# A graph network kernel: the second edge sort is cut into counts, blocks beside the attention pass, and blocks behind it

## What is computed

```python
xn = layernorm(x)
# layer 0: sum over the edges at their source
agg0 = segment_sum(xn[dst] * edge_weight[:, None], src, num_segments=6250)
x = x + relu((xn + agg0) @ W1 + b1) @ W2 + b2 + linear_attention(xn)
x = x + expert_ffn(layernorm(x))
# layer 1: sum over the edges at their target
xn = layernorm(x)
agg1 = zeros.at[dst].add(xn[src])
x = x + (deg_isqrt * agg1) @ W + attention_layers(xn)
x = x + mixture_of_experts(x)
```

## Time and profile before

| what | us |
|---|---|
| median of the three runs | 6170.95 |
| the profiled execution: its own time | 6176.16 |
| its span in the trace | 6174.4 |
| the first sort's scatters on POOL, first and last start | 53.3, 1201.1 |
| DVE free of all earlier work | 1187.1 |
| the records landed, DVE goes on | 1207.82 |
| first gather of the first message stage | 1211.72 |

### The profile page before, as it was taken

One profiled execution on the slowest core, in us unless ns is written; L12 is line 12 of the kernel. 1 busy time (PEld: TensorE's weight loads), 2 busy tenths in 40 slices (PEclk: granted clock), 3 DMA queues, 4 the chain that ended last, 5 costly groups with the idle time before them and its releaser, 6 DMA issues.

```text
span 6174.4 us, 88136 instructions
## 1 busy us (share of the span) xinstructions
PE 5219.2 (85%) x24825; PEld 4400.5 (71%) x24825; DVE 3351.4 (54%) x9920; ACT 1347.2 (22%) x3057; POOL 3934.7 (64%) x4345
## 2 busy tenths in 40 slices
PE   0255667389999999989999899899999999997698
PEld 0154555267777777778888788687888878886587
DVE  9867666545555555547344634464454654445632
ACT  0011111011111111124223422142111421111254
POOL 5777777765555555588888887405767046763555
PEclk9977788699999999999999999999999999999899
DMA  1022222233333333711001100213333124354454
GB/s 44 24 72 83 57 57 67 74 109 97 102 98 98 98 101 97 91 40 53 14 17 28 50 16 21 72 44 96 106 99 99 58 86 118 111 103 119 127 93 73
DMA packets 323178, 465.05 MB, mean 75 GB/s; under 512 B 98998, under 2 KB 253050, under 8 KB 322866
## 3 DMA queue, kind: packets, MB, share of 16 engines
q0 software_dynamic: 163312, 261.71, 18.4%
q1 hardware_dynamic: 159554, 199.67, 10.8%
HBM read 359.22 MB, written 102.61 MB: 75 GB/s over the span
## 4 chain that ended last, share of the span: by engine, by line
PE 69%; DMA 10%; DVE 8%; POOL 7%; issue 4%; ACT 1%; DVEq 0%; SPq 0%; POOLq 0%; ACTq 0%
PE bank L2379 19%; PE bank L2390 14%; DMA scratch_sorted<-sb_FREE 7%; POOL scratch_sorted L1028 6%; PE bank L2425 6%; PE bank L2607 6%; PE bank L2440 5%; PE bank L2589 5%; PE bank L2873 3%; PE bank L2732 3%; DMA sb_rows<-scratch_xn,sb_row_of 3%; PE bank L2370 2%; PE bank L2915 1%; DVE sb_STATE L1511 1%; PE bank L2584 1%
## 5 line engine op out<-in xcount | busy, mean ns | idle before, releaser
L1035 POOL DMA_INDIRECT sb_rows<-scratch_xn,sb_row_of x1760 | 1718.3, 976 | 1437.9 <-PE bank L2425 608.9
L1028 POOL DMA_INDIRECT scratch_sorted<-sb_FREE x1564 | 1605.3, 1026 | 486.4 <-issue 329.8
L2390 PE MATMUL bank<-sb_work_FT,sb_W 128*128 128x250 f32 x4400 | 1010.4, 381 | 20.1 <-ACT sb_work_FT L1115 15.6
L1115 ACT ACTIVATE sb_HT<-bank,sb_cols 128x250 f32<-128x250 f32 x1333 | 553.8, 467 | 1986.5 <-PE bank L2589 1062.0
L2390 PEld LDWEIGHTS bank<-sb_work_FT,sb_W 128*128 128x128 f32 x4400 | 848.0, 194 | 135.9 <-ACT sb_work_FT L1115 23.2
L2379 PE MATMUL bank<-sb_W,sb_HT 128*125 128x256 f32 x4000 | 893.4, 380 | 0.7 <-ACT sb_HT L1115 0.7
L2379 PEld LDWEIGHTS bank<-sb_W,sb_HT 128*125 128x125 f32 x4000 | 752.4, 188 | 114.9 <-ACT sb_HT L1115 1.1
L2440 PE MATMUL bank<-sb_rows,sb_work_TM 128*125 128x257 f32 x1760 | 468.2, 389 | 70.0 <-DMA sb_rows<-scratch_xn,sb_row_of 68.3
L1780 DVE TENSOR_TENSOR sb_FREE<-sb_FREE,bank 125x257 f32 x440 | 186.1, 423 | 624.2 <-PE bank L2425 589.0
L1835 DVE TENSOR_TENSOR sb_STATE<-sb_STATE,bank 125x257 f32 x440 | 185.8, 422 | 621.3 <-PE bank L2440 590.7
L2425 PE MATMUL bank<-sb_rows,sb_work_TM 128*125 128x257 f32 x1760 | 441.7, 390 | 37.4 <-DMA sb_rows<-scratch_xn,sb_row_of 27.8
(11 more groups left out here) (390 smaller groups left out, 7042.3 us busy)
## 6 DMA issues: line engine op xcount, KB each, us to landing
sb_rows<-scratch_xn,sb_row_of POOLq DMA_INDIRECT x1760, 2.8
scratch_sorted<-sb_FREE POOLq DMA_INDIRECT x1564, 2.4
scratch_qT<-sb_work_QF SPq DMA_DIRECT2D x100, 250.0 KB
sb_work_QF<-scratch_qT SPq DMA_DIRECT2D x100, 250.0 KB
sb_HT<-scratch_zs SPq DMA_DIRECT2D x54, 261.0 KB, 3.1
sb_work_XC<-in_x SPq DMA_DIRECT2D x50, 250.0 KB
sb_work_ZT<-scratch_xn SPq DMA_DIRECT2D x50, 250.0 KB
sb_W<-in_L_mix_W SPq DMA_DIRECT2D x9, 1024.0 KB
```

The costliest lines, as they stand in the source:

```text
L1028: nc.gpsimd.indirect_dma_start(out=sorted_d[e], out_offset=bass.IndirectOffsetOnAxis(ap=pos[e][0:n, c:c + 1], axis=0), in_=rec[e][0:n, 2 * ...
L1035: nc.gpsimd.indirect_dma_start(out=rows[:, t % RING, 0:D], out_offset=None, in_=table, in_offset=bass.IndirectOffsetOnAxis(ap=row_of[:, t: ...
L1115: return nc.scalar.activation(dst, source, func, **k)
L2390: ins = nc.tensor.matmul(dst[:, b, :], w[:, k0 + k, 128 * (b0 + b):128 * (b0 + b) + 128], source[:, k, :], start=(n == 0), stop=(n == 2 * ...
```

## The change

The second sort gets its ranks as the first sort's rest does: for each block a mask, a running sum from `base`, a predicated copy. This needs `base` first, so the first pass makes only counts, and the ranks come later.

- In `A0` each of the 25 `sort_rank` becomes `sort_second_count`: one product with a sum. The places in the turn stay.
- Between the passes the six operations on the ranks go; `base` is copied to a buffer of its own (`base_kept`), and the places (`at_kept`) are cleared. In the preparation two memsets of 782 columns go.
- In `B0` the 25 `sort_start` go. `sort_second_place(i, n)` handles two blocks a turn, 26 in 13 turns: n = 0 to 2 (two masks, the first running sum) behind "m" and ahead of the next turn's begin; n = 3 to 5 (the second running sum, two predicated copies) where the second `sort_start` stood.
- Behind `B0` comes `sort_blocks(1)`, then the other 24 blocks, two at a time, then six operations that make slots of places, where there were one addition and five such operations.
- `VT` is now a view of a buffer on 128 partitions, which the counts reuse. Instructions of PE, ACT, POOL and SP keep their order.

```diff
+        blk_kept, at_kept, is_kept, counts_kept = blk, rank, [is_b, lane], [scan, tmp]
+        base_kept = sb("base_kept", [128, NT])
...
+        BESIDE = 2 * NP
...
             def sort_prepare_second():
...
                 step(nc.vector.memset(f1, 1.0))
-                step(nc.vector.memset(rank, 0.0))
-                step(nc.vector.memset(tmp, 0.0))
+
+            def sort_second_count(k):
+
+                dve.wait_ge(sort_step, k + SECOND_READY)
+                nc.vector.scalar_tensor_tensor(is_b, half, iota_b[:, bass.ds(k, 1)], step_of, ALU.is_equal, ALU.mult,
+                                               accum_out=packed[:, bass.ds(k, 1)]).then_inc(sort_step, 1)
+
+            def sort_second_counted():
+
+                dve.wait_ge(sort_step, SECOND_COUNTED - 3)
+                decode_counts(steps(SECOND_COUNTED - 3))
+
+            def sort_second_keep():
+
+                dve.wait_ge(sort_step, SECOND_KEPT - 1)
+                nc.vector.memset(at_kept, 0.0).then_inc(sort_step, 1)
+
+            def sort_second_place(c, n):
+
+                j, stage = n % 2, n // 2
+                b = 2 * c + j
...
+                if stage == 2:
+                    hold(dve)
+                if stage == 0:
+                    ins = nc.vector.tensor_scalar(is_kept[j], blk_kept, iota_b[:, bass.ds(b, 1)], None, ALU.is_equal)
+                elif stage == 1:
+                    ins = nc.vector.tensor_tensor_scan(counts_kept[j], is_kept[j], is_kept[j], base_kept[:, bass.ds(b, 1)],
+                                                       ALU.add, ALU.max)
+                else:
+                    ins = nc.vector.copy_predicated(at_kept, is_kept[j].bitcast(I32), counts_kept[j])
+                ins.then_inc(sort_step, 1)
...
             def body_a0(i, slots, after):
                 if after:
                     begin_a0(i + 1, after)
-                rank_beside(i, 0)
+                count_beside(i, 0)
...
-                rank_beside(i, 1)
+                count_beside(i, 1)
...
             make_context("A0")
-            sort_decode(1)
+            sort_second_counted()
             sort_groups(1)
+            sort_second_keep()
...
                     normed(s, TM[s], ptok(PB[s]), 1).then_inc(*dve_done.add("B0", "m", slots, s))
+                for n in range(3):
+                    sort_second_place(i, n)
                 if after:
                     begin_b0(i + 1, after)
-                start_beside(i, 0)
...
-                start_beside(i, 1)
+                for n in range(3, 6):
+                    sort_second_place(i, n)
...
             pairs_next(dve, begin_b0, body_b0)
-            sort_place_second()
             sort_blocks(1)
-            dve.wait_ge(sort_step, SORT_END)
+            for c in range(NP, NT // 2):
+                for n in range(6):
+                    sort_second_place(c, n)
+            sort_second_slots()
+            dve.wait_ge(sort_step, SECOND_PLACED)
```

More of the change, by code:

```diff
@@ L352, in build @@
         work = {n: sb("work_" + n, [128, 2, 512]) for n in ("XC", "ZT", "QT", "KT", "TM", "FT", "QF")}
-        VT = sb("VT", [T, 2, 2, 2, 129])
+        VT_all = sb("VT", [128, 2, 2, 2, 129])
+        VT = VT_all[0:T, :, :, :, :]
         HT = sb("HT", [128, 2, 8, CH])
@@ L1417, in sort_prepare_second @@
                 f0, f1 = fields_of(1)
-                step = steps(SORT_BASE[1])
+                step = steps(SECOND_BEGUN)
                 blocks_of_keys(step, dst_i)
@@ new lines, in sort_second_keep @@
+            def sort_second_keep():
[4 more added lines that the diff above has]
+                b = 2 * c + j
+                rest = isinstance(c, int) and b >= BESIDE
+                begun = (SECOND_REST - 3 * BESIDE if rest else SECOND_KEPT) + n
+                fresh = n == 0 and (first(c) or (rest and b == BESIDE))
+                dve.wait_ge(sort_step, c * 6 + (begun if n == 5 or fresh else begun - 1))
+                if stage == 2:
[8 more added lines that the diff above has]
+                ins.then_inc(sort_step, 1)
@@ new lines, in sort_second_slots @@
+            def sort_second_slots():
+                dve.wait_ge(sort_step, SECOND_PLACED - 6)
+                step, at, slot = steps(SECOND_PLACED - 6), at_kept, is_kept[0]
+                step(nc.vector.tensor_scalar(at, at, -1.0, None, ALU.add))
+                step(nc.vector.tensor_scalar(slot, at, 63.5, 1.0 / 128, ALU.subtract, ALU.mult))
+                step(nc.vector.tensor_scalar(slot, slot, ROUND, ROUND, ALU.add, ALU.subtract))
+                step(nc.vector.scalar_tensor_tensor(at, slot, -128.0, at, ALU.mult, ALU.add))
+                step(nc.vector.scalar_tensor_tensor(at, at, float(NS), slot, ALU.mult, ALU.add))
+                step(nc.vector.tensor_copy(pos[1], at))
@@ L1457, in decode_counts, with slots_placed @@
                 step(nc.vector.scalar_tensor_tensor(first_of, second_of, -SECOND, both_of, ALU.mult, ALU.add))
-            def slots_placed(step, e, columns):
+            def slots_placed(step, columns):
                 at, slot = (x[:, columns] for x in (start, lane))
@@ L1465, in slots_placed @@
                 step(nc.vector.scalar_tensor_tensor(at, at, float(NS), slot, ALU.mult, ALU.add))
-                step(nc.vector.tensor_copy(pos[e][:, columns], at))
+                step(nc.vector.tensor_copy(pos[0][:, columns], at))
             def sort_first_strips():
@@ L1486, in sort_first_strips @@
                     step(nc.vector.tensor_reduce(start[:, columns], strip_own.rearrange("p b c -> p c b"), AX.X, ALU.add))
-                    slots_placed(step, 0, columns)
+                    slots_placed(step, columns)
             def sort_first_rest():
@@ L1518, in sort_first_rest @@
                 dve.wait_ge(sort_step, FIRST_PLACED - 5)
-                slots_placed(steps(FIRST_PLACED - 5), 0, columns)
-            def sort_rank(e, k):
-                before = SORT_BASE[e] + PREPARED
-                dve.wait_ge(sort_step, k * 4 + before)
-                nc.vector.scalar_tensor_tensor(is_b, half, iota_b[:, bass.ds(k, 1)], step_of, ALU.is_equal, ALU.mult)\
-                    .then_inc(sort_step, 1)
-                dve.wait_ge(sort_step, k * 4 + (before + 1))
-                nc.vector.tensor_tensor_scan(scan, is_b, tmp, 0.0, ALU.add, ALU.add).then_inc(sort_step, 1)
-                dve.wait_ge(sort_step, k * 4 + (before + 2))
-                nc.vector.tensor_copy(packed[:, bass.ds(k, 1)], scan[:, EC - 1:EC]).then_inc(sort_step, 1)
-                hold(dve)
-                nc.vector.copy_predicated(rank, is_b.bitcast(I32), scan).then_inc(sort_step, 1)
-            def sort_decode(e):
-                dve.wait_ge(sort_step, SORT_BASE[e] + RANKED)
-                step = steps(SORT_BASE[e] + RANKED)
-                decode_counts(step)
-                step(nc.vector.tensor_scalar(is_b, rank, *HIGH, ALU.subtract, ALU.mult))
-                step(nc.vector.tensor_scalar(is_b, is_b, ROUND, ROUND, ALU.add, ALU.subtract))
-                step(nc.vector.scalar_tensor_tensor(rank, is_b, -SECOND, rank, ALU.mult, ALU.add))
-                step(nc.vector.tensor_tensor(is_b, is_b, rank, ALU.subtract))
-                step(nc.vector.tensor_tensor(is_b, is_b, odd, ALU.mult))
-                step(nc.vector.tensor_tensor(rank, rank, is_b, ALU.add))
+                slots_placed(steps(FIRST_PLACED - 5), columns)
             def sort_groups(e):
```

58 lines of the change are left out of this document (20 added, 38 removed).

## The result

The changed kernel takes 6188.76 us, the median of nine runs (6182.71 to 6199.84). The kernel before takes 6170.95 in as many (6168.45 to 6176.54). The ratio is 1.0026, with a 95% interval of 1.0017 to 1.0035: slower, by 18 us of medians, and 4 us above the range of 6159 to 6185. The profiled execution of the changed kernel spans 6186.4 us, 12.0 more than that of before; its first gather is 13.9 us later and what lies behind it is 1.9 shorter. What follows explains these 13.9; the rest of the 18 comes from which executions were profiled (that of before took 5.2 more than its median, that of the changed kernel 0.6 less).

The account below looks back on a forecast made before the run. POOL's scatters bound the first gather, with 20.7 us of room on DVE. DVE gains 60 us and pays 78, free at 1205; records land at 1206, 2 us earlier: 6169 us on the median's scale, range 6159 to 6185.

Parts of the forecast that it names:

- First pass, 35.2 us: First attention pass on DVE: twelve rank steps on the path become one product with a sum, each saving 2.93 us.
- the step behind the context sum: Second rank step of a first-pass turn: stands in DVE's wait for the next x, so shortening it only lengthens the wait.
- Preparation 1.9 and between the passes 2.7: Ahead of the first pass two memsets go, 1.9 us; between the passes six rank operations go, 2.7 us net.
- Second pass, 20 us by PE's room: Ten second-pass turns each gain the smaller of DVE's 2.5 us and PE's room: 20 us, bounds 0 and 25.
- Behind the pass, 24 x 3.25: Behind the second pass: 24 added blocks of mask, scan and copy at 3.25 us each, 78 us, bounds 76 and 84.
- The scatters, net -2: POOL's scatters ahead of the first gather: 3.4 us lost beside the blocks, passes' share included; records at 1206, before 1207.8.
- the bound of 6: Most the scatters could lose beside the 24 blocks and what follows, in us, against 3.4 forecast and 0 at least.
- The passes' share: Scatters during the shorter passes: 0 us won if their toll goes with transfers, 6 us if it goes with time.
- The masks starve the scatters: Rival: each 0.6 us mask holds POOL for its whole length, records at 1222, a run of 6185; chance 0.03.
- The ranks end last: Rival: second pass gains nothing, blocks cost 3.5 us, DVE free at 1231, gather 23 us late, 6193; chance 0.11.
- scatters go faster: Rival: with fewer scans and copies in the first pass, records land 15 us early, a run of 6157; chance 0.06.
- The sum: First gather at the later of DVE 1205 and records 1206, 2 us before 1207.8: 6169 us, no measurable change, chance 0.80.

## Why the prediction was wrong

- **First pass, 35.2 us.** Right: the pass ends 36.7 us sooner measured from its begin (340.1 before, 303.4 after), and the step behind the context sum only lengthened the wait for x, as said.
- **Preparation 1.9 and between the passes 2.7.** Right: the first pass begins at 259.77 instead of 261.67, and from the end of one pass to the begin of the next it is 14.2 instead of 17.4.
- **Second pass, 20 us by PE's room.** Right: 524.2 instead of 544.8, 20.6. PE is next, as said, by the 1.30 us of waiting ahead of the second tile's statistics.
- **Behind the pass, 24 x 3.25.** Right: 3.35 each. DVE is free at 1204.83 for 1205, since 2.4 us more won in the passes cancel 2.5 more in the blocks.
- **The scatters, net -2.** Here it failed. "The 24 blocks and what follows take some 87 us at 37 in 50 where the open rate gives 38.5: 2.6 scatters, 3.4 us lost" was to be 20 us lost, and the bound of 6 didn't hold it. The step took a rate from blocks of 2.66 us and used it for blocks of 3.35, as if the toll grew with time. It is what a block lasts beyond the two scatters that fall into step with it, 0.13 at 2.66 us and 0.83 at 3.35; it comes from scatters that start in a running sum or a copy and go on only at its end, and 2.66 us is the shortest block measured, with the least toll. The earlier trace rows had the sign of it: a longest scatter of 3.178 beside a median of 0.958. The passes' share was forecast at 0 to 6 us won and gave 5.
- **The rivals.** "The masks starve the scatters" named the place, and its chance was 0.03. That its time of 6185 is close is luck: it has every mask hold POOL for its whole length, and in the changed kernel's blocks behind the pass no mask held a scatter for more than 0.04 us; the sums and copies did. That a mask holds a scatter which starts in it is right all the same (103 of 103, 0.14 to 0.42 us each). The Trainium skill, SBUF — State Buffer, section Who interferes with whom, which the prediction drew on for two-port operations, also states that a DVE instruction with two inputs from SBUF contends with a GpSimd instruction that reads SBUF. That sentence was the one to weigh, and the traces agree with it: beside running sums the scatters took 1.433 us, and beside sums with one operand in PSUM 0.958. "The ranks end last" and "scatters go faster" didn't happen.
- **The sum.** 14 us for a net -2 of scatters turned "no change that can be measured" into 0.26% slower.

## What to carry to other kernels

Where two engines race to one point, work that is added to the one that has room is free only if it doesn't slow the other: look for the longest instance of the other's instruction, not only its median, and see beside what it stands. A rate read in one stretch carries over to another only if the operations there have the same length, since an engine that is held falls into step with the one that holds it. For the same reason a run in which nothing is held shows only where the starts fell: look at when each operation starts before you call it harmless. And before work is moved into a stretch, try what else binds there: here one number, the scatters in flight, was worth more than the change, and the wait for q had room for half as many blocks again.

## What was not expected of the hardware

- A scatter of GpSimd that started well inside a running sum, a predicated copy or a mask on SBUF tensors ended 0.76 to 0.84 us behind that operation (in rows of short copies or of additions, and in a few other cases, behind a later one); a free one takes 0.96, also beside sums with one operand in PSUM.
- 132 masks in a row fell into step with the scatters: these started within 0.02 us of a mask's start and took 0.96, and every second mask took 0.81 us instead of 0.62.
- Held scatters lock to the DVE sequence: 0.96 and 1.09 in each block of 2.66 us, 1.19 and 1.39 in each of 3.18, the same two per block.
- It goes the other way too: beside POOL's select two DVE operations on one tensor took 2.13 us instead of 0.57.
- Scatters landed after 5.2 us (median) in the first pass with eight in flight; with four, POOL waited 66 us there for landings.
